# Norms of q and k from Gram matrices, and one folded projection in place of two projections and their maps

## The chip, the cores and the metric

The kernel runs on one core of one Trainium2 chip. The metric is the time of one execution on the device, in microseconds: the median of several runs. Profiles are of one execution, taken by the hardware profiler; their span runs from the first to the last instruction and is a little shorter than the time of the same execution.

## What is computed

A graph layer over 2500 nodes of 1024 features: normalise the rows of x, add to x a graph convolution (a sparse 2500 x 2500 matrix of 42500 weighted edges times xn @ W) and a mixing term, and then a feed-forward block with ternary weights. The change is in the mixing term:

```python
def _L0_mix_ref(x, Wq, bq, Wk, bk, Wv, bv, weights):      # x: normalised rows
    q = (x @ Wq.T + bq).reshape(Bx, Sx, H, D)              # 16 heads of 64
    k = (x @ Wk.T + bk).reshape(Bx, Sx, H, D)
    v = (x @ Wv.T + bv).reshape(Bx, Sx, H, D)
    q = q / jnp.linalg.norm(q)                             # one norm over the whole tensor
    k = k / jnp.linalg.norm(k)
    def phi(t):
        sq_norm = jnp.sum(t * t)
        scale = jnp.exp(-sq_norm / 2) / jnp.sqrt(jnp.float32(M))
        return jnp.exp(jnp.einsum('hmd,bshd->bshm', weights, t)) * scale
    phi_q = phi(q)
    phi_k = phi(k)
    s = jnp.einsum('bshm,bshm->bsh', phi_q, phi_k)[..., None]
    out = s * v / s
```

The norms are single numbers, so |q|^2 is a sum over all entries of (xn' xn) times (Wq' Wq), with the bias as one more column. And phi_q times phi_k is one exponential of the sum of both maps, so once the norms are known, map, projection and norm of q and of k can be folded into one 1024 x 1024 matrix.

## The kernel before

A tile is 125 rows of x (TILES = 20); KT = 8 blocks of 128 features. Matrix products in fp32 accuracy are made of three fp32r products, of a high and a low part of each operand (product3: lines 333, 334, 335). The high part is a copy on ACT, the low part a subtraction on DVE, 1 to 1.2 us for a tile each. PE takes its work strictly in the written order, as do ACT, DVE, POOL and SP (which issues most DMAs); semaphores tie them.

Stage 1 (0 to 107 us): SP loads x, DVE takes the row statistics (L952) and scales the rows (L963), PE transposes them (L1277), ACT copies the transposed tile into one of four slots of XT (L724), SP writes it out as xnT (L428). A slot is free when its store has landed. Stage 2 (to 627 us): groups of four tiles (500 rows) come back as xg. For q, then for k, for each of 5 groups and 8 blocks of heads: 24 products of 500 columns give a block of q (PS banks 4 and 5), ACT adds the bias, makes its high part and the sum of its squares (L761, L762), DVE the low part (L1000), three products with the block-diagonal maps bdH, bdL follow one block later (maps), and ACT and SP write the result u to DRAM (uT). The weights Wq and Wk are transposed by PE in the same stretch. Then the norms, a few tiny operations in a chain. Stage 3 (to 894 us): per tile 48 products of 512 columns give xn @ W (tile_products), kept in S; beside it u of q and k come back (uu), ACT takes exponentials, DVE multiplies, and PE sums over the 64 maps with eight products of 2 columns (map_sums, L1382) into s_all. Stage 4 (to 1146 us): Wv is loaded and transposed, v for each tile, times s, over s. Stage 5 (to 1707 us): the graph convolution as a dense product with A, which is read back from DRAM. Stage 6: the feed-forward block.

Beside stages 1 to 4, the dense A is built: POOL fills two matrices with zeros (40 strips of 1280 KB, L682), DVE compares the keys of each pair of 128-edge chunks (edge_pair, L345 to L350: four operations, 168 pairs) to sum edges that fall on one cell, and POOL scatters the sums with 336 indirect DMAs (L698), alternating between the two matrices; a matrix takes its next pair once its last has landed. Before stage 5 all of it must be done.

Of the kernel before, what the change touches and what calls it, by code (L numbers as in the profile page):

```python
# [32 lines left out]
P = 128  # L33
# [21 lines left out]
AHEAD = 2  # L55
PER_IT = 4
ITERS = 2 * GROUPS
BLOCKS = AHEAD + PER_IT * ITERS
CHUNKS = BLOCKS * CH_BLOCK
ROWS_C = CHUNKS  # L60
assert CHUNKS * P >= EDGES
CT = ROWS_C // 4

# [4 lines left out]
S_AT = W_AT + 2 * 4 * KT * D  # L68
# [11 lines left out]
def layer_kernel(nc, x, src, dst, edge_weight, W, Wq, bq, Wk, bk, Wv, bv, mix_w, w_gate, w_up, w_down, out):  # L80
# [5 lines left out]
    uT_d = nc.dram_tensor("uT", (2, P, KT, NODES), F32).ap()  # L86
# [22 lines left out]
    sel = small("sel", [P, 2])  # L109
    eps = small("eps", [P, 1])  # L110
    neg_round = small("neg_round", [P, 1])
    bqk = small("bqk", [P, 2, KT])
# [5 lines left out]
    ssq = small("ssq", [P, 2 * GROUPS * KT])  # L118
# [27 lines left out]
    w1 = zone("W1", W_AT, S_AT)  # L146
    XT = w1("XT", [P, GT, KT, ROWS])
    iedge = w1("iedge", [P, 2, ROWS_C], I32)
    kT_sb = w1("kT_sb", [P, 8, P])


    X = zone("S1", S_AT, E_AT)("X", [P, TILES, D])
    s2 = zone("S2", S_AT, E_AT)
    xg = s2("xg", [P, GT, KT, ROWS])
    xgH = s2("xgH", [P, 2, KT, GN], F32R)
    xgL = s2("xgL", [P, 2, KT, GN], F32R)
    S = zone("S3", S_AT, E_AT)("S", [P, TILES, D])


    e1 = zone("E1", E_AT, END_AT)  # L160
    wst = e1("wst", [P, 2, D])
# [3 lines left out]
    bdH = e1("bdH", [P, KT, P], F32R)  # L165
    bdL = e1("bdL", [P, KT, P], F32R)
    at = cursor["E1"]
    XN = zone("E1a", at, END_AT)("XN", [P, 2, D])
    e1b = zone("E1b", at, END_AT)
    qH = e1b("qH", [P, 2, GN], F32R)  # L170
    qL = e1b("qL", [P, 2, GN], F32R)
    usb = e1b("usb", [P, 2, GN])
    zeros = e1b("zeros", [P, A_PITCH // 4])
    squares = e1b("squares", [P, 2, GN], BF16)


    zx = zone("E2x", E_AT, END_AT)("zx", [P, 2, D])
# [4 lines left out]
    bvb = e2("bvb", [P, D])  # L182
    rows2 = zone("E2r", cursor["E2"] - 4 * D, END_AT)("rows2", [P, D])
    at = cursor["E2"]
    e2a = zone("E2a", at, END_AT)
    uu = e2a("uu", [P, 2, 2, 2, GN])
    rows3 = zone("E2s", cursor["E2a"] - 4 * 4 * GN, END_AT)("rows3", [P, 2, D])
    e2b = zone("E2b", at, END_AT)
    rs_all = e2b("rs_all", [P, TILES, HEADS])
# [3 lines left out]

# [8 lines left out]
    rq16 = e3("rq16", [P, TILES, D], BF16)  # L202
    Araw = e3("Araw", [P, 2, GN])
    AH = [e3(f"AH{i}", [P, GN], F32R) for i in range(2)]
    AL = [e3(f"AL{i}", [P, GN], F32R) for i in range(2)]

# [28 lines left out]
    Q_BLOCKS = ITERS * KT // 2  # L235
# [13 lines left out]
    s_exp = sems("s_exp", 2)  # L249
# [1310 lines left out]
```

## Time and profile before

| | us |
|---|---|
| median of 3 runs | 1879.35 |
| lowest, highest | 1879.14, 1879.56 |
| the profiled execution | 1875.68 |
| its span | 1873.9 |
| TensorE busy in the span | 1739.3 |
| VectorE (DVE) busy | 1101.7 |
| ScalarE (ACT) busy | 652.7 |
| GpSimd (POOL) busy | 578.4 |

PE is the matmul row, PEld the loads of its stationary operand, which overlap it. "Granted clock" is TensorE's clock as a share of 2.4 GHz; the other of its two levels is 1.2 GHz. Matmuls are pipelined, so the distance between two starts is what one costs, not its duration. A time in square brackets behind a row is how long the engine was idle before it, and what released it. A DMA share of 1 means that all 16 DMA engines were occupied.

### The profile page before, as it was taken

Reading aid. Unit: us, or ns where it says so; the run is one execution under the profiler, and the core shown is the slowest. Engines: PE = TensorE matmul, PEld = TensorE weight load, DVE = VectorE, ACT = ScalarE, POOL = GpSimd, SP = SyncE. Lnnn points to the kernel's source line nnn. Section 1 sums busy time; section 2 is a strip of 40 time slices with the busy share of each in tenths; the row PEclk is TensorE's granted clock in tenths of the full one; section 3 lists DMA queues with packets and bytes.
Section 4 is the critical chain, followed back from the end, with each engine's and each line's share of the span. In section 5 each row is a group of like instructions: output and inputs, shape, how many; then the busy total and the mean of one; then the engine's idle time right before and its main releaser. Section 6 shows DMA issues by size and latency. Waiting matters only on the chain.

```text
span 1873.9 us, 25902 instructions
## 1 busy us (share of the span) xinstructions
PE 1739.3 (93%) x8020; PEld 1390.9 (74%) x8020; DVE 1101.7 (59%) x2583; ACT 652.7 (35%) x937; POOL 578.4 (31%) x392
## 2 busy tenths in 40 slices
PE   2379999999999899999799999899999999999797
PEld 2368788888888688888677777677777777777465
DVE  5476777877777622222456664448566584755765
ACT  1243333443333533333322221223333343333443
POOL 1011111277787787877766700000000000000000
PEclk9689999999999899999999999899999999999899
DMA  8989999976666745545787756524545344453355
GB/s 204 324 353 379 384 382 380 380 189 164 160 161 165 233 99 131 124 107 132 182 247 212 201 176 178 163 90 140 131 131 139 91 142 131 131 142 99 113 165 160
DMA packets 176137, 356.75 MB, mean 190 GB/s; under 512 B 63979, under 2 KB 112139, under 8 KB 176091
## 3 DMA queue, kind: packets, MB, share of 16 engines
q1 hardware_dynamic: 109591, 278.48, 46.1%
q0 software_dynamic: 59264, 52.62, 13.0%
q10 hardware_dynamic: 7236, 25.12, 4.6%
q8 instruction: 19, 0.31, 0.1%
q14 instruction: 27, 0.22, 0.0%
HBM read 238.62 MB, written 117.53 MB: 190 GB/s over the span
## 4 chain that ended last, share of the span: by engine, by line
PE 82%; DMA 6%; DVE 5%; SPq 3%; ACT 2%; issue 1%; POOL 0%; ACTq 0%; DVEq 0%; POOLq 0%
PE PS L333 25%; PE PS L335 25%; PE PS L334 24%; PE PS L1493 4%; PE PS L1518 2%; DMA uT<-usb 2%; PE PS L1382 2%; DMA xnT<-XT 1%; PE PS L1277 1%; SPq L77 1%; SPq L417 1%; DMA ewrow<-weight_rows 1%; DMA Aside<-A_dense 1%; DVE junk L345 1%; ACT hqT L904 1%
## 5 line engine op out<-in xcount | busy, mean ns | idle before, releaser
L698 POOL DMA_INDIRECT A_dense<-wtot,cell x336 | 541.9, 1613 | 183.2 <-issue 100.7
L333 PE MATMUL PS<-SL,AH 125*125 125x512 f32 x800 | 317.6, 397 | 12.0 <-DVE AL L1133 11.9
L335 PE MATMUL PS<-SH,AH 125*125 125x512 f32 x800 | 318.0, 397 | 0.0
L334 PE MATMUL PS<-SH,AL 125*125 125x512 f32 x800 | 316.2, 395 | 0.0
L333 PE MATMUL PS<-WL,xtH 128*125 128x512 f32 x640 | 257.0, 402 | 4.8 <-DVE WL L1068 2.7
L333 PE MATMUL PS<-xgL,WH 128*128 (+1 forms) x640 | 250.7, 392 | 4.7 <-issue 4.7
L335 PE MATMUL PS<-WH,xtH 128*125 128x512 f32 x640 | 253.6, 396 | 0.0
L334 PE MATMUL PS<-WH,xtL 128*125 128x512 f32 x640 | 252.8, 395 | 0.0
L334 PE MATMUL PS<-xgH,WL 128*128 (+1 forms) x640 | 250.0, 391 | 0.0
L335 PE MATMUL PS<-xgH,WH 128*128 (+1 forms) x640 | 249.6, 390 | 0.0
L1130 DVE TENSOR_TENSOR SL<-S,SH 125x1024 fp32r<-125x1024 f32 x100 | 122.3, 1223 | 169.9 <-ACT SH L843 169.9
L843 ACT ACTIVATE SH<-S 125x1024 fp32r (+1 forms) x100 | 106.0, 1060 | 315.7 <-PE PS L335 315.7
L333 PEld LDWEIGHTS PS<-SL,AH 125*125 125x125 f32 x800 | 149.1, 186 | 50.7 <-DVE AL L1133 14.1
L334 PEld LDWEIGHTS PS<-SH,AL 125*125 125x125 f32 x800 | 149.3, 187 | 38.9
L335 PEld LDWEIGHTS PS<-SH,AH 125*125 125x125 f32 x800 | 149.3, 187 | 38.1
L345 DVE SCALAR_TENSOR_TENSOR junk<-keyrow,key,ewrow 128x256 bf16<-128x256 f32 x336 | 148.7, 479 | 4.1 <-DMA ewrow<-weight_rows 4.1
L761 ACT ACTIVATE qH<-PS,bqk 128x500 fp32r<-128x500 f32 x80 | 54.2, 678 | 267.2 <-PE PS L335 267.2
L333 PEld LDWEIGHTS PS<-WL,xtH 128*125 128x125 f32 x640 | 119.6, 187 | 33.7 <-issue 4.9
L333 PEld LDWEIGHTS PS<-xgL,WH 128*128 128x128 f32 x640 | 121.4, 190 | 30.1 <-issue 4.9
L335 PEld LDWEIGHTS PS<-WH,xtH 128*125 128x125 f32 x640 | 119.3, 186 | 30.1
L334 PEld LDWEIGHTS PS<-WH,xtL 128*125 128x125 f32 x640 | 119.8, 187 | 28.3
L335 PEld LDWEIGHTS PS<-xgH,WH 128*128 128x128 f32 x640 | 121.1, 189 | 25.2
(149 smaller groups left out, 2224.8 us busy)
## 6 DMA issues: line engine op xcount, KB each, us to landing
A_dense<-zeros POOLq DMA_DIRECT2D x40, 1280.0 KB, 11.0
Araw<-A_dense SPq DMA_DIRECT2D x100, 250.0 KB, 2.7
Aside<-A_dense SPq DMA_DIRECT2D x100, 250.0 KB, 2.9
xg<-xnT SPq DMA_DIRECT2D x11, 2000.0 KB, 14.1
uu<-uT SPq DMA_DIRECT2D x44, 500.0 KB, 4.5
keyrow<-key_rows SPq DMA_DIRECT2D x42, 512.0 KB, 4.9
ewrow<-weight_rows SPq DMA_DIRECT2D x42, 512.0 KB, 6.9
xt<-xnT SPq DMA_DIRECT2D x42, 500.0 KB, 5.1
```

The source lines that it names most:

```text
L77: eng.dma_start(dst[cut:ROWS], src[cut:ROWS]).then_inc(sem, 16)
L333: nc.tensor.matmul(o, lh, rl, start=start, stop=False)
L334: nc.tensor.matmul(o, ll, rh, start=False, stop=False)
L335: return nc.tensor.matmul(o, lh, rh, start=False, stop=stop)
L345: nc.vector.scalar_tensor_tensor(junk[:, slot, 2 * c:2 * c + 2, :].rearrange("p a n -> p (a n)"), row, key[:, col], wrow, ALU.is_equal, AL ...
L698: pool.indirect_dma_start(cells[m], bass.IndirectOffsetOnAxis(cell[:, col:col + 1], 0), wtot[:, col:col + 1], None, compute_op=ALU.add).th ...
L761: nc.scalar.activation(qH[:, j % 2, :], PS[:, 4 + j % 2, 0:GN], ACT.Identity, bias=bias)
L843: nc.scalar.activation(SH[0:ROWS, i, :], S[0:ROWS, bass.ds(s, 1), :].rearrange("p o n -> p (o n)"), ACT.Copy).then_inc(s_s[i], 1)
L1130: nc.vector.tensor_tensor(SL[0:ROWS, i, :], S[0:ROWS, bass.ds(s, 1), :].rearrange("p o n -> p (o n)"), SH[0:ROWS, i, :].bitcast(F32), ALU. ...
L1382: last = nc.tensor.matmul(PS[0:ROWS, 4 + jj, 2 * d:2 * d + 2], uu[:, i, jj, 0, d * ROWS:(d + 1) * ROWS], sel[:, :], start=True, stop=True)
L1493: last = nc.tensor.matmul(PS[0:ROWS, 2 * i + c, :], rqT[:, i, k, 0:ROWS], wT[:, c, :, k * P:(k + 1) * P], start=k == 0, stop=k == KT - 1)
L1518: last = nc.tensor.matmul(PS[0:ROWS, 4 + c, :], hqT[:, i, k, 0:ROWS], down_blocks(c, k), start=k == 0, stop=k == INNER // P - 1)
```

## The change

1. Stage 1 keeps the scaled rows in X and makes, right behind each tile's transposes, the left half of the Gram matrix xn' xn (gram with G_LEFT, banks 0 to 3; only blocks on and above the diagonal, with two more columns for the sums of the columns). High and low parts of a tile lie in ring, three slots. A second pass over the 20 tiles makes the right half (G_RIGHT). ACT copies the banks to Gs.
2. The same for the rows of Wq and Wk (raw, split in high and low parts into split), untransposed; DVE multiplies those banks with Gs and sums (weigh), which gives both norms.
3. The maps, scaled by the norms (bdqk), times the rows of Wq and Wk give one matrix: 128 + 16 fp32 products (fold), into TH and TL.
4. One more pass of tile_products with TH and TL, in front of W's, gives the exponents of both maps together; DVE adds the bias, ACT takes the exponential, DVE sums over each head. u, uT, uu, xg, the maps' products and map_sums are gone.
5. The order around it: SP loads x first and the biases as rows of 512 bytes; POOL starts its strips of zeros at once (four free, then one per Gram item), twenty pairs of edges go to A[0] alone while A[1] is zeroed; the edge pairs on DVE follow a table of pairs per step; the rows of Wv come in parts, the most of them during the last tiles of W's pass.

The core of the diff:

```diff
+G_LEFT = [(0, 0, 512, 0, 0), (0, 512, 1024, 1, 0), (1, 128, 640, 2, 0), (1, 640, EXT, 3, 0), (0, D, EXT, 3, 386)]
+G_RIGHT = [(2, 256, 768, 0, 0), (2, 768, EXT, 1, 0), (7, 896, EXT, 1, 258), (4, D, EXT, 1, 388), (3, 384, 896, 2, 0),
+           (3, 896, EXT, 3, 0), (6, 768, EXT, 3, 130), (4, 512, 1024, 4, 0), (5, 640, EXT, 5, 0)]
+EDGE_PLAN = [1] * TILES + [0, 0, 0, 0, 1, 1, 1, 1] + [0, 1, 1, 0, 1, 1, 0, 1] + [1, 0, 1, 0, 1, 0, 1, 1] \
+    + [1, 1, 1, 1, 1, 1, 0, 0] + [4] + [2] * KT + [3] * (TILES - KT) + [4] * 18 + [0] * 2
...
     @block.sync
+        sp.wait_ge(s_st, 6)
+        for n in range(6):
+            load_raw(n, s_raw[0])
         for t in range(TILES):
             sp.wait_ge(s_xev[t % 2], t // 2 + 1)
             sp.dma_start(xnT_d[t].rearrange("p k r -> p (k r)"), XT[:, t % GT].rearrange("p k r -> p (k r)")).then_inc(s_xTout[t % GT], 16)
...
     @block.gpsimd
+        for r in range(STRIPS):
+            if r >= 4:
+                pool.wait_ge(s_gm, r - 3)
+            zero_strip(0, r)
+        for i in range(2):
+            pool.wait_ge(s_Azero[i], 16 * (STRIPS // 2))
+        for r in range(STRIPS):
+            zero_strip(1, r)
+            scatter_pair(r, 0)
...
     @block.scalar
+        for n in range(TILES):
+            if n % 2 == 0 and n + 2 < TILES:
+                deviations(n // 2 + 1)
+            high_of_rows(n + 1)
+            transposed_rows(n)
...
     @block.vector
+        dve.wait_ge(s_gm, ITEMS)
+        weigh(1, K_RIGHT, RIGHT_WIDTHS, 4)
...
+        for t in range(TILES):
+            i = t % 2
+            low_of_tile(1 - i, t // 2 + i)
+            if t < KT:
+                dve.wait_ge(s_w2h, t + 1)
+                nc.vector.tensor_tensor(WL[:, t, :], stage[:, t % 2, :], WH[:, t, :].bitcast(F32), ALU.subtract).then_inc(s_w2l, 1)
+            dve.wait_ge(s_mm[i], t // 2 + 1)
+            if t >= 2:
+                dve.wait_ge(s_red[i], t // 2)
+            nc.vector.tensor_tensor(ex[0:ROWS, i, :], two_banks(i)[0:ROWS], bb[0:ROWS, :], ALU.add).then_inc(s_ta[i], 1)
+            edges(STEP_T + t)
+            dve.wait_ge(s_ex[i], t // 2 + 1)
+            nc.vector.tensor_reduce(s_all[0:ROWS, t, :], ex[0:ROWS, i, :].rearrange("p (h n) -> p h n", h=HEADS), AX.X,
+                                    ALU.add).then_inc(s_red[i], 1)
...
     @block.tensor
+        def gram(segments, banks, hi, lo, first, last_one):
+            opened = set()
+            for i, a, b, bank, at in segments:
+                o = PS[:, banks[bank], at:at + b - a]
+                cols = slice(i * P, (i + 1) * P)
+                nc.tensor.matmul(o, hi[:, cols], lo[:, a:b], start=first and bank not in opened, stop=False, skip_group_check=True)
+                opened.add(bank)
+                nc.tensor.matmul(o, lo[:, cols], hi[:, a:b], start=False, stop=False, skip_group_check=True)
+                last = nc.tensor.matmul(o, hi[:, cols], hi[:, a:b], start=False, stop=last_one, skip_group_check=True)
+            last.then_inc(s_gm, 1)
...
+        def fold(lhs_of, rows, slot):
+            for j in range(KT):
+                for m in range(2):
+                    last = nc.tensor.matmul(by_block(two_banks(2 + slot))[0:rows, j, :], lhs_of(m * KT + j), bdqk[:, m, j, :],
+                                            start=m == 0, stop=m == 1)
+            last.then_inc(s_fold, 1)
...
+        with pe.Fori(0, HALF) as h:
+            for i in range(2):
+                pe.wait_ge(s_xtl[i], h + 1)
+                pe.wait_ge(s_ta[i], h)
+                tile_products(i, TH, TL)
```

On PE, the transposes of stage 1 stand before in a loop over pairs of tiles, and the transposes of two weight blocks and the products of stage 2 follow once it is done (XN is the scaled tile, wst two slots for rows of a weight matrix, xgH, xgL and WH, WL the parts of four tiles and of the weights):

```order
L1277 MATMUL PS<-ident_49,XN_95 128x128 x16
L1291 REGISTER_ALU
L1291 COMPARE_AND_BRANCH
L1277 MATMUL PS<-ident_49,wst_89 128x128 x16
L333 MATMUL PS<-xgL_87,WH_79 128x500
L334 MATMUL PS<-xgH_86,WL_80 128x500
L335 MATMUL PS<-xgH_86,WH_79 128x500
```

In the changed kernel, PE's first tile reads so, and the next follows at once:

```order
L1294 MATMUL PS<-ident_49,X_85 128x125 x8
...
L1281 MATMUL PS<-ring_83 128x512
L1278 MATMUL PS<-ring_83 128x386
L1280 MATMUL PS<-ring_83 128x386
L1281 MATMUL PS<-ring_83 128x386
L1278 MATMUL PS<-ring_83 128x2
L1280 MATMUL PS<-ring_83 128x2
L1281 MATMUL PS<-ring_83 128x2
L1294 MATMUL PS<-ident_49,X_85 128x125 x8
```

Fifteen Gram products stand now between the transposes of two tiles, and three of them have 2 columns.

On SP before, between the last loads of x and the first keys' rows:

```order
L76 DMA X<-in_x 112x4x1024
L77 DMA X<-in_x 13x4x1024
L417 DMA bqk<-in_L_mix_bq 128x8x1
L417 DMA bqk<-in_L_mix_bk 128x8x1
L391 DMA wst<-in_L_mix_Wq 128x1024 [waits s_tr0]
L391 DMA wst<-in_L_mix_Wq 128x1024
L428 DMA xnT<-XT 128x1000 [waits s_xev0]
```

And in the changed kernel:

```order
L97 DMA X<-in_x 112x2x1024
L98 DMA X<-in_x 13x2x1024
L437 DMA raw<-in_L_mix_Wq 128x1024 [waits s_st]
L437 DMA raw<-in_L_mix_Wq 128x1024 x5
L445 DMA xnT<-XT 128x1000 [waits s_xev0]
```

The first store of xnT still stands behind all of x; in between stand six weight blocks where two were, and the biases have moved up in front of the fourth pair of tiles.

On PE again, what stands between the last Gram product and the first tile of the added pass (norms are the two sums, earlier a block of ones, brow the folded bias):

```order
L1281 MATMUL PS<-split 128x386
L1344 MATMUL PS<-norms,earlier 128x2
L1349 MATMUL PS<-bdqk,raw 128x128 x128
L1349 MATMUL PS<-bdqk,raw 2x128 x16
L1365 MATMUL PS<-brow,earlier 128x512 x2
```

Nothing of PE's other work is left to stand beside the norms: the fold reads the scaled maps, and the pass behind it the folded matrix.

## Rows read from the trace of the kernel before

**Rows 1.** The page: the span, and shares of the chain that ended last.

```profile
span 1873.9 us, 25902 instructions
...
PE 82%; DMA 6%; DVE 5%; SPq 3%; ACT 2%; issue 1%; POOL 0%; ACTq 0%; DVEq 0%; POOLq 0%
```

**Rows 2.** By stretch: length; busy PE, PEld, DVE, ACT, POOL; clock; DMA share; GB/s.

```profile
30.00:60.00 30.00, 8.52 (x45) 7.85 (x43) 15.32 (x31) 4.21 (x5) 0.00 (x0) 0.67 0.93 207
60.00:107.00 47.00, 23.79 (x128) 21.22 (x129) 26.14 (x45) 22.11 (x25) 2.38 (x3) 0.68 0.87 331
...
200.00:320.00 120.00, 119.91 (x530) 99.33 (x529) 88.48 (x377) 43.32 (x85) 14.24 (x20) 1.00 0.99 379
```

**Rows 3.** The same view in stretches of 10 us.

```profile
20.00:30.00 10.00, 1.08 (x5) 1.08 (x6) 6.98 (x15) 1.58 (x2) 0.00 (x0) 1.00 1.05 250
...
110.00:120.00 10.00, 10.00 (x46) 8.33 (x45) 9.86 (x55) 2.26 (x4) 0.71 (x1) 0.90 1.02 417
```

**Rows 4.** Timeline of stage 1: start, length, engine, operation, idle before and releaser.

```profile
20.83 4.84 DVE L952 BATCH_NORM_STATS2 stats<-X 125x6 f32<-125x512 f32 x8 [5.67 <-DMA X<-in_x]
...
33.05 18.03 SPq L417 DMA_DIRECT2D bqk<-in_L_mix_bk  x1
...
57.77 2.37 SPq L428 DMA_DIRECT2D xnT<-XT  x4
...
64.34 1.00 ACT L724 ACTIVATE XT<-PS 128x1000 f32<-128x1000 f32 x1 [25.34 <-DMA xnT<-XT]
```

**Rows 5.** Timeline of PE in stage 2, five products apart.

```profile
616.71 0.39 PE L333 MATMUL PS<-xgL,WH 128*128 x1
...
617.84 0.38 PE L335 MATMUL PS<-xgH,WH 128*128 x1
```

**Rows 6.** Timeline of PE in stage 3, around the map sums of a tile.

```profile
653.79 0.39 PE L333 MATMUL PS<-WL,xtH 128*125 128x512 f32 x1
...
660.72 1.80 PE L1382 MATMUL PS<-sel,uu 128*125 128x2 f32 x16
...
662.38 0.48 PE L333 MATMUL PS<-WL,xtH 128*125 128x512 f32 x1
```

**Rows 7.** The chain in order of time: start, length, work.

```profile
137.08 0.81 DVE junk L345 x4
138.56 0.81 DVE junk L345 x4
...
326.75 0.88 PE PS L1277 x8
...
660.88 1.64 PE PS L1382 x16
673.76 1.64 PE PS L1382 x16
```

**Rows 8.** Groups by line: operands, count, busy us, mean ns, idle before.

```profile
L1130 DVE TENSOR_TENSOR SL<-S,SH 125x1024 fp32r<-125x1024 f32 x100 | 122.3, 1223 | 169.9 <-ACT SH L843 169.9
...
L1000 DVE SCALAR_TENSOR_TENSOR qL<-PS,bqk,qH 128x500 fp32r<-128x500 f32 x80 | 58.9, 736 | 82.2 <-ACT squares L762 82.1
...
L963 DVE TENSOR_SCALAR XN<-X,mv,rstd 125x1024 f32<-125x1024 f32 x20 | 15.8, 811 | 9.3 <-PE PS L1277 9.1
...
L1356 PE MATMUL PS<-norms,earlier 128*128 128x2 f32 x2 | 0.5, 330 | 3.2 <-DVE norms L1030 3.2
```

**Rows 9.** Timeline of PE from the last map sums to the first product of v.

```profile
894.46 1.94 PE L1277 MATMUL PS<-ident,wst 128*128 128x128 f32 x16 [0.52 <-issue]
...
903.82 3.63 PE L1277 MATMUL PS<-ident,rows 128*128 128x128 f32 x16 [4.76 <-DMA rows<-in_L_mix_Wv]
...
909.07 0.47 PE L333 MATMUL PS<-WL,xtH 128*125 128x512 f32 x1
```

**Rows 10.** All scatters of POOL: count, ns min/median/max, first and last start.

```profile
L698 POOL DMA_INDIRECT A_dense<-wtot,cell x336: 1538/1541/2557, 362.1 to 1073.9; - x168
```

**Rows 11.** DMA issues, the strips of zeros: count, KB each, us to landing.

```profile
A_dense<-zeros POOLq DMA_DIRECT2D x40, 1280.0 KB, 11.0
```

More of the change, by code:

```diff
@@ L477, in load_tile, with load_w_rows @@
+        next_key_rows(0, STEP_Q)
+        sp.wait_ge(s_gm, G_ITEMS)
+        for n in range(10, 2 * KT):
+            load_raw(n, s_raw[2])
+        def load_w_rows(k):
+            sp.dma_start(stage[:, k % 2, :], W[k * P:(k + 1) * P, :]).then_inc(s_stage[k % 2], 16)
+        sp.wait_ge(s_lo, G_ITEMS)
+        for k in range(2):
+            load_w_rows(k)
+        next_key_rows(STEP_Q, STEP_FOLD)
         def load_tile(t, i):
@@ L702, in _ @@
+        for pair in range(ALONE, BLOCKS * PAIRS):
+            scatter_pair(pair, (pair + 1) % 2)
     @block.scalar
     def _(act):
[L704 to L709 removed]
@@ L777, in _ @@
-        stage2_group(0, 0, own=True)
-        with act.Fori(1, GROUPS - 1) as g:
-            stage2_group(0, g)
-        stage2_group(0, GROUPS - 1, ahead=True)
-        stage2_group(1, 0)
-        with act.Fori(1, GROUPS) as g:
-            stage2_group(1, g)
-        evacuate_u(ITERS - 1, KT - 1)
+        act.wait_ge(s_ev0, 4)
+        nc.scalar.activation(raw[:, 0:KT, D:EXT], bias[:, 0], ACT.Copy).then_inc(s_ev0, 1)
+        act.wait_ge(s_ev0, 5)
+        act.wait_ge(s_lo, G_ITEMS)
+        for j in range(2):
+            high_of_weights(0, j)
@@ new lines, in _ @@
+        act.wait_ge(s_gm, G_ITEMS)
+        evacuate_gram(RIGHT_BANKS, RIGHT_SCALES, 4, (0, 1))
+        high_of_weights(0, 2)
+        evacuate_gram(RIGHT_BANKS, RIGHT_SCALES, 4, (2, 3))
+        high_of_weights(0, 3)
+        evacuate_gram(RIGHT_BANKS, RIGHT_SCALES, 4, (4, 5))
+        nc.scalar.activation(raw[:, KT:2 * KT, D:EXT], bias[:, 1], ACT.Copy).then_inc(s_ev0, 1)
+        for j in range(4, KT):
+            high_of_weights(0, j)
+        act.wait_ge(s_ev0, 6)
+        for j in range(KT):
+            high_of_weights(1, j)
@@ new lines, in _ @@
+        for j in range(KT):
+            edges(STEP_K + j)
+        dve.wait_ge(s_gm, G_ITEMS + 3 * KT)
+        weigh(1, K_LEFT, LEFT_WIDTHS, 0)
+        for j in range(KT):
+            edges(STEP_K + KT + j)
+        dve.wait_ge(s_gm, ITEMS)
+        weigh(1, K_RIGHT, RIGHT_WIDTHS, 4)
+        dve.wait_ge(s_bs, 20)
+        dve.wait_ge(s_rs, 2)
+        nc.vector.tensor_reduce(norms[:, 0, :], parts[:, :, :], AX.X, ALU.add).then_inc(s_norm, 1)
+        dve.wait_ge(s_norm, 3)
+        nc.vector.reciprocal(norms[:, 2, :], norms[:, 1, :]).then_inc(s_norm, 1)
@@ new lines, in _ @@
+        pe.wait_ge(s_bdq, 2)
+        for k in range(KT):
+            if k == 1:
+                pe.wait_ge(s_norm, 5)
+            if k >= 2:
+                pe.wait_ge(s_fl, k - 1)
+            fold(lambda n: raw[:, n, k * P:(k + 1) * P], P, k % 2)
+        pe.wait_ge(s_fl, KT - 1)
+        fold(lambda n: raw[:, n, D:EXT], 2, 0)
+        pe.wait_ge(s_fl, KT)
+        pe.wait_ge(s_bb, 1)
+        for c in range(2):
+            last = nc.tensor.matmul(PS[:, 6 + c, :], earlier[0:1, 0, :], brow[0:1, c * 512:(c + 1) * 512], start=True, stop=True)
```

928 lines of the change are left out of this document (416 added, 512 removed).

## The prediction

> **What bounds the kernel now.** I read the page first: the chain that ended last is PE for 82% of the span of 1873.9 us [rows 1]. So time is gained only where PE does less or waits less. The table by stretch then says where it waits: busy for 8.5 of the 30 us from 30 to 60 and 23.8 of the 47 us from 60 to 107, at a granted clock of 0.67 and 0.68, against 119.9 of 120 us at 1.00 (the 2.4 GHz level) from 200 to 320 [rows 2]. So there are two prices: PE time after 107 us counts in full, PE time before it is mostly free. Why the first 107 us are idle shows in the timeline: the first xnT store goes out at 57.77, behind all of x and two bias loads that hold SP's queue for 18 us, and ACT copies tile 4 only at 64.34 [rows 4].
>
> **Unit prices.** Products of 500 columns start 0.226 us apart (616.71 to 617.84, five steps) [rows 5], of 512 columns 0.231 (653.79 to 660.72, 30 products) [rows 6]. Between them the width alone acts, so I price 386 columns at 0.178 and 258 at 0.125 (500 less the columns at 2.4 GHz). The trace shows no fp32r product under 500 columns. Below, its bound is a weight load alone: 16 records of 2 columns take 1.66 us, 0.104 each [rows 6]; above, the price of a 512-column one, 0.231. For 2 columns I take 0.104, for 130 columns 0.11, the price of a transpose of 128 columns (8 in 0.88 us) [rows 7]. The page "TensorE: Matmul & The Clock Gate" of the Trainium skill (section "Back-to-back issue gap") gives 81 ns for a streamed product of 128 columns; by it the 216 products of 130 columns would cost 6 us less in all; the transposes here show 110 ns, and the sum goes by them.
>
> **The change, part by part.** I compare one milestone: the start of the first transpose of Wv, now at 894.46 [rows 9]. Behind it the program is the same but for one wait.
>
> *Left Gram pass over x, in stage 1.* Per tile 15 products: 3 x (3 x 0.231 + 0.178 + 0.104) = 2.93 us, with 8 transposes 3.81. DVE needs per tile 1.21 (statistics, 8 in 4.84 [rows 4]) + 0.81 (scaling) + 1.22 (low part) [rows 8] = 3.3, ACT two copies of 1.0 [rows 4]: both under PE. But the first xnT store again stands last in SP's queue: x (10.24 MB at 235 to 250 GB/s [rows 3], 43 us) and six weight blocks (3.1 MB, 8 to 12 us), so it lands no sooner than 55 to 58. Beside it POOL now zeroes A from the start: ten strips may go before tile 6, 1.31 MB each [rows 11], 3.1 us at 417 GB/s [rows 3], up to 31 us of the same engines. ACT waits for that landing at tile 4, and PE at tile 6 waits for ACT. The stall ends between 57 and 88; I take 72, about the middle. From there 14 tiles x 3.81 = 53, and 7 for a cold start and the chain through ACT: the pass ends at **132** (117 to 148). The section "Queues, rings and completion order" of "DMA: Bandwidth & Descriptors" in the Trainium skill says that a DMA engine takes turns between queues, packet by packet; by it the strips get their full share and the pass ends near 148. No row of before has x and strips together.
>
> *Right pass.* Per tile 27 products: 3 x (3 x 0.231 + 2 x 0.125 + 2 x 0.11 + 0.104 + 0.178) = 4.34; 20 tiles are **86.8**, after 1.8 us in which ACT empties two banks. DVE's share per tile, 1.22 [rows 8] and an edge pair of 1.5 us (137.08 to 138.56 [rows 7]), hides.
>
> *Gram of the weights.* Twice 8 x (2.93 + 4.34): **116.3**. In front of each of the four parts PE waits for banks: 2.0 (ACT), 1.8 (two weighings at 0.74 [rows 8]), 5.3 (last high part on ACT 1.0 [rows 4], low 1.22, an edge pair 1.5, two weighings), 2.2: **11.3**.
>
> *Norms.* Six weighings of about 0.69, reduction, ones product, root, reciprocal and two scalings of the maps at 0.8 (as the scaling of a tile [rows 8]): **8.0**, all with PE idle.
>
> *Folding.* 144 fp32 products of 128 columns, each two records as in L1356 (x2) [rows 8]: from 2 x 0.104 to 2 x 0.231. I take 0.225, two transposes: 32.4, and 4 for the cold clock, 3 for the bias row: **39.3** (to 73 at the upper bound).
>
> *Projection.* 20 x 48 = 960 products more, at 0.232: **222.5**, and W's own pass **222.5** now that the map sums are gone from it (a tile took 12.88 us, 660.88 to 673.76 [rows 7]). DVE has about 8.5 us of work per tile beside 11.1 (three edge pairs, 4.5, and three whole-tile operations and flags, 4.0): it hides, but with two more edge pairs it would set the pace.
>
> Sum: 132 + 1.8 + 86.8 + 116.3 + 11.3 + 8.0 + 39.3 + 445 + 0.5 = **841**, against 894.5: 53.5 us. What this replaces is not listed apart; it is all that stands between 107 and 894.46, above all 2160 products of 500 columns (488 us) and 33 us of map sums.
>
> *Boundary to Wv.* PE waits 4.76 us for rows [rows 9]; now rows 2 to 6 come during the last two tiles of W, since uu no longer takes the room. That wait and a little of the rhythm behind it go: 5.5. What is late next is DVE's 1.22 per block, already in the rhythm.
>
> *Scatter.* 336 scatters took from 362.1 to 1073.9 [rows 10], 2.12 us each. Now the first pairs follow at about 150, but twenty of them go to one matrix and alternate with strips; while W's pass runs, DVE offers 72 pairs faster (four per tile of 11.1) than POOL takes them (4.24 each), so POOL ends about 305 us behind the start of that pass at 616, near 920. The loads of A stand in front of the last two tiles of v, near 1065: it hides, with 140 us to spare.
>
> The whole: 53.5 + 5.5 = 59 us. The profiled execution took 1875.68 (span 1873.9), so 1816.7; the median of before, 1879.35, lies 3.7 above that execution: **1820**.
>
> **Rivals.** (a) *Products of 130 columns cost four passes*, as fp32 takes more than one record for its product: 0.234 in place of 0.11, 216 times: 27 us, **1847**. For it: nothing narrow in fp32r is in the trace. Against it: the transposes. (b) *Four passes up to 258 columns too*: 216 x (0.124 + 0.323) = 96.5 us, **1916**. This is the way to end slower. The price is PE's alone, in right passes over x and weights; it decides as soon as the narrow products together cost 59 us more than I charge, which 130 columns alone can't reach and 258 do. Against it: from 512 to 500 columns the price falls with the width. (c) *The DMA stall in stage 1 is not there*: x and strips overlap, xnT lands before PE needs tile 6, the pass ends at 99: **1787**. For it: 417 GB/s are moved from 110 to 120 us, x alone moves 250, so engines that look full have room. Against: x alone showed a share of 1.05.
>
> **How the numbers follow.** Forecast 0.56, (a) 0.25, (b) 0.05, (c) 0.12, the fold at its upper bound or a wait that I overlook by itself 0.02 beyond the range. The range, 1794 to 1860, takes in pass ends from 117 to 148 and rival (a) with some of the fold's upper bound; most of (c) and all of (b) are left out. A difference of about 0.2% (4 us) is what a measurement can tell from none. Faster 0.93: all but (b) and a little. Same 0.01, slower 0.06.
>
> **What would show it.** Spacing of the products by width: 512 at 0.231, 258 at 0.125, 130 at 0.11 (a right item at 4.34, a left one at 2.93). ACT's wait for xnT at its fifth copy, ending near 72, and PE idle from about 45 to 75. The first product of W's pass near 616, the first transpose of Wv near 841. The fold's 128 products in 29 us. POOL's last scatter before the loads of A. I am wrong where a right item takes over 5 us, where the stall goes or lasts beyond 88, or where tiles of the projection take over 11.3 us because DVE or the loads of xt come late.

## The result, and the profile after

| | before | after |
|---|---|---|
| median of 4 executions, us | 1879.24 (1879.09 to 1879.56) | 1820.91 (1818.56 to 1824.12) |
| profiled execution, its time / its span, us | 1875.68 / 1873.9 | 1823.07 / 1821.3 |
| PE busy in it | 1739.3 us (93%) | 1705.3 us (94%) |
| instructions | 25902 | 23768 |

The ratio is 0.969 (95% interval 0.967 to 0.971): 58.3 us less by the medians. By the profiled executions it is 52.6 us of span, since that of before lay 3.6 us under its median and that of after 2.2 us above its own. The steps below are compared within the profiled executions.

The page of after: the span, PE in 40 slices of 45.5 us with the granted clock, and the engines of the chain that ended last; it answers [rows 1].

```profile
span 1821.3 us, 23768 instructions
...
PE   5199998899999999999999997999999999999797
...
PEclk9599999999999999999999998999999999999899
...
PE 88%; DMA 3%; DVE 3%; SPq 3%; issue 1%; ACT 1%; DVEq 0%; ACTq 0%
```

PE's share of the chain rose from 82% to 88%. Apart from the first slice, in which the first rows arrive, the one hole is in the second: "1" for PE, "5" (the 1.2 GHz level) for its clock. By stretch (length; busy PE, PEld, DVE, ACT, POOL; clock; DMA share; GB/s), to be held against [rows 2]:

```profile
30.00:46.00 16.00, 14.70 (x93) 13.01 (x92) 9.03 (x16) 5.57 (x8) 1.67 (x2) 1.00 1.02 414
46.00:83.00 37.00, 0.82 (x7) 0.74 (x5) 1.34 (x4) 2.46 (x3) 3.35 (x4) 0.54 0.99 393
83.00:140.00 57.00, 56.23 (x324) 50.07 (x324) 43.13 (x73) 30.46 (x39) 7.54 (x9) 0.94 0.91 348
141.00:228.00 87.00, 87.00 (x540) 78.90 (x540) 53.47 (x178) 21.86 (x24) 43.12 (x30) 1.00 0.82 270
403.00:850.00 447.00, 447.00 (x1924) 357.25 (x1925) 300.70 (x1157) 86.58 (x89) 310.38 (x196) 1.00 0.55 132
```

From 46 to 83 us no engine is busy for more than a tenth of the time (PE for 0.82 of 37 us), while the DMA engines are full. In the right pass (141 to 228) and in the two passes over 20 tiles (403 to 850) PE is busy all the time. The hole in the timeline of stage 1 (start, length, engine, line, operation, idle before and what ended it), as [rows 4] showed it for before:

```profile
37.26 14.96 SPq L437 DMA_DIRECT2D raw<-in_L_mix_Wq  x6
...
52.26 34.80 SPq L445 DMA_DIRECT2D xnT<-XT  x7
80.54 1.00 ACT L698 ACTIVATE XT<-PS 128x1000 f32<-128x1000 f32 x1 [39.25 <-DMA xnT<-XT]
...
83.74 1.93 PE L1294 MATMUL PS<-ident,X 125*128 125x125 f32 x8
```

The first xnT store leaves SP's queue at 52.26, behind x and the six raw weight blocks, and lands 28 us later. ACT's fifth copy waits for it, PE for that copy. What shared the DMA engines, by queue from 46 to 81 us (packets, MB, share of the 16 engines; q1 is SP's queue, q0 the queue of POOL, which zeroes A):

```profile
q1 hardware_dynamic: 2058, 7.44, 53.3%
q0 software_dynamic: 1638, 6.38, 45.3%
```

The price of a product by its width, from an item of the right pass: three products each of 512, 258, 130 and 2 columns.

```profile
180.63 0.40 PE L1281 MATMUL PS<-ring 125*128 125x512 f32 x1
180.87 0.28 PE L1278 MATMUL PS<-ring 125*128 125x258 f32 x1
...
181.22 0.23 PE L1278 MATMUL PS<-ring 125*128 125x130 f32 x1
181.28 0.28 PE L1280 MATMUL PS<-ring 125*128 125x130 f32 x1
181.40 0.28 PE L1281 MATMUL PS<-ring 125*128 125x130 f32 x1
181.51 0.22 PE L1278 MATMUL PS<-ring 125*128 125x2 f32 x1
...
181.81 0.48 PE L1278 MATMUL PS<-ring 125*128 125x512 f32 x1
182.13 0.39 PE L1280 MATMUL PS<-ring 125*128 125x512 f32 x1
182.36 0.40 PE L1281 MATMUL PS<-ring 125*128 125x512 f32 x1
...
184.50 0.39 PE L1278 MATMUL PS<-ring 125*128 125x512 f32 x1
```

Three of 258 columns take 0.35 us from start to start (0.118 each), three of 130 columns 0.29 (0.097), three of 2 columns 0.30 (0.10). The average of three hides how they lie: over the 35 triples of 130 columns in this pass the second product starts 0.06 us behind the first, and the next two starts follow at 0.110 and 0.112 to 0.113 (0.28 us in all); behind the first of three products of 2 columns the distances are 0.079, 0.112 and 0.112. So from 130 down to 2 columns the distance no longer falls. Where the 258 columns follow 130, their three take 0.41 us instead of 0.35. The item ends at 184.50, 4.33 us after its first product at 180.17. The first 512-column product behind the narrow ones holds the next one back to 0.32 us.

Last, the boundary to Wv, against [rows 9], and the scatters, against [rows 10]:

```profile
849.65 1.91 PE L1269 MATMUL PS<-ident,zx 128*128 128x128 f32 x16
853.29 2.19 PE L1269 MATMUL PS<-ident,keyrow 128*128 128x128 f32 x16 [1.73 <-DVE WL L1062]
...
858.77 0.47 PE L354 MATMUL PS<-WL,xtH 128*125 128x512 f32 x1
```

```profile
L662 POOL DMA_INDIRECT A_dense<-wtot,cell x336: 1533/1542/2517, 157.3 to 988.9; - x168
```

The 4.76 us wait for rows is gone; two waits for DVE (1.73 and 1.34 us) stand in this stretch. The last scatter starts at 989 instead of 1074.

### The profile page after: what moved, and what is told of

It reads as the page before. It is cut to its first block, busy times and chain, and to the rows that moved or that the text cites. A ratio compares the mean times of both kernels' runs of the same rounds, so it can differ in the third digit from the quotient of the medians.

```text
span 1821.3 us, 23768 instructions
## 1 busy us (share of the span) xinstructions
PE 1705.3 (94%) x8178; PEld 1372.3 (75%) x8178; DVE 1097.2 (60%) x2537; ACT 513.7 (28%) x610; POOL 580.5 (32%) x392
## 4 chain that ended last, share of the span: by engine, by line
PE 88%; DMA 3%; DVE 3%; SPq 3%; issue 1%; ACT 1%; DVEq 0%; ACTq 0%
PE PS L356 22%; PE PS L355 22%; PE PS L354 22%; PE PS L1280 5%; PE PS L1278 5%; PE PS L1281 5%; PE PS L1491 4%; PE PS L1516 2%; PE PS L1349 2%; DMA xnT<-XT 2%; DMA Aside<-A_dense 1%; SPq L98 1%; SPq L437 1%; PE PS L1294 1%; ACT hqT L884 1%
## 5 line engine op out<-in xcount | busy, mean ns | idle before, releaser
L354 PE MATMUL PS<-WL,xtH 128*125 128x512 f32 x640 | 252.6, 395 | 2.7 <-DVE WL L1062 2.7
L355 PEld LDWEIGHTS PS<-SH,AL 125*125 125x125 f32 x800 | 149.6, 187 | 37.4
L354 PE MATMUL PS<-TL,xtH 128*125 128x512 f32 x320 | 127.1, 397 | 0.0
L356 PE MATMUL PS<-TH,xtH 128*125 128x512 f32 x320 | 126.9, 397 | 0.0
L355 PE MATMUL PS<-TH,xtL 128*125 128x512 f32 x320 | 126.3, 395 | 0.0
L1022 DVE TENSOR_TENSOR xtL<-xt,xtH 128x1000 fp32r<-128x1000 f32 x61 | 73.1, 1198 | 75.1 <-ACT xtH L767 74.6
L1278 PE MATMUL PS<-ring 125*128 125x512 f32 (+4 forms) x280 | 95.4, 341 | 4.8 <-DVE ring L934 3.4
L934 DVE TENSOR_TENSOR ring<-X,ring 125x1024 fp32r<-125x1024 f32 x40 | 48.7, 1217 | 84.7 <-ACT ring L692 84.7
```

The source lines that it names most:

```text
L354: nc.tensor.matmul(o, lh, rl, start=start, stop=False)
L355: nc.tensor.matmul(o, ll, rh, start=False, stop=False)
L356: return nc.tensor.matmul(o, lh, rh, start=False, stop=stop)
L1022: nc.vector.tensor_tensor(xtL[i][:, :, :], xt[:, i], xtH[i][:, :, :].bitcast(F32), ALU.subtract).then_inc(s_xtl[i], 1)
L1278: nc.tensor.matmul(o, hi[:, cols], lo[:, a:b], start=first and bank not in opened, stop=False, skip_group_check=True)
```

## The experiments

All times are medians. The kernel before stood beside every group at 1879 to 1880 us.

**The base, once more.** No edit.

> The changed kernel as it is, as the base of this group. Both theories: 1818 to 1824 us, PE idle from about 47 to about 83 us in stage 1, the store of tile 0 landing near 80 us. A question beside it: its runs so far lie near 1818.6 or near 1823.5 us; if the difference sits in one stage, a second profile should show that stage 4 to 5 us shorter or longer than the first.

Measured: 1824.0 us (1820.4 to 1824.6), 3.1 above the median of the first group. The hole lies at the same place, but ACT waits until 82.8 instead of 80.5, and the left pass ends 1.9 us later. This profile again fell among the longer executions, so what shortens the others by 4 to 5 us isn't seen in one. Their mean granted clock is 0.977 to 0.978 against 0.974 to 0.975; the clock experiment below comes back to it.

**Who delays the store: three edits.** First, the strips of zeros wait for the left pass:

```diff
-            if r >= 4:
-                pool.wait_ge(s_gm, r - 3)
+            pool.wait_ge(s_gm, max(7, r - 3))
```

> The zero strips of the first half of A from number 4 on wait until left tile 7 is through PE (before: strip r waits for left tile r-4), so that GpSimd's queue moves nothing in 52 to 81 us. The queue of the strips moved 6.38 of 14.10 MB in 46 to 81 us. Theory (the store waits behind what shares the DMA engines with it): q1 alone moves what stands ahead of the store, some 6 MB, at up to 400 GB/s, so the store of tile 0 lands near 65 to 70 us instead of 80, and the time falls by 10 to 15 us, to about 1808. Rival (q1 by itself is no faster than with the strips beside it: in 10 to 30 us, before the strips, it moved 324 to 344 GB/s or less): it lands at 72 or later and the gain is under 8 us.

Measured: 1806.3 us, 17.7 less than the base. Timeline of ACT, then 50 to 60 us by stretch:

```profile
62.86 1.00 ACT L697 ACTIVATE XT<-PS 128x1000 f32<-128x1000 f32 x1 [22.41 <-DMA xnT<-XT]
```

```profile
50.00:60.00 10.00, 0.00 (x0) 0.00 (x0) 0.00 (x0) 0.00 (x0) 0.00 (x0) 0.50 1.01 360
```

The store lands 18 to 20 us sooner, for two reasons: it is issued at 40.6 instead of 52 to 54 us (SP's own issues get through faster), and then needs 22 instead of 28 us. The rival falls: SP's queue alone moved 3.44 of the 3.60 MB of this stretch, 344 GB/s, 1.6 times the 213 GB/s (7.44 MB in 35 us) that it had beside the strips. So the strips cost the changed kernel some 18 us; I had expected 10 to 15. One number of the expectation was misread: the 324 to 344 GB/s in 10 to 30 us of the changed kernel were not SP's queue before the strips, since the strips moved 3.40 of the 6.68 MB there.

Second, the six raw weight blocks go behind the loop of the stores:

```diff
-        for n in range(6):
-            load_raw(n, s_raw[0])
         for t in range(TILES):
...
             sp.wait_ge(s_xTout[i], 16 * GROUPS)
+        for n in range(6):
+            load_raw(n, s_raw[0])
         for n in range(6, 10):
```

> The six raw weight loads (3.1 MB) are issued behind all stores of x tiles instead of ahead of them. Theory (bytes ahead in SP's queue set the landing): at 210 GB/s for q1 beside the strips, 3.1 MB are 15 us, so the store of tile 0 lands near 65 us, and the time falls by 12 to 15 us, to about 1807. Rival (SP's issue of the raw loads, 37 to 52 us, is what delayed the store, not their bytes): the store is issued at about 42 instead of 52 us and still takes 28 us: it lands near 70, a gain of about 10 us. Second rival (the rest of stage 1 then runs into the late weights): the gain is lost again before the Q projection's Gram pass, total within 3 us of the base.

Measured: 1812.4 us (1804.9 to 1817.2), 11.6 less. The store is issued at 37.5 and lands at 66.2, as long under way (29 us) as before. It lands where the theory put it, its flight is that of the first rival: the two are not told apart. The second rival falls: PE waited for no load in the Gram pass of the weights. That pass did take 134.2 us from the start of its first product to that of its last, against 129.0 in the base, at a mean clock of 0.92 against 0.96, a matter taken up below.

Third, the stores leave SP's queue:

```diff
@@ sync
-            sp.wait_ge(s_xev[t % 2], t // 2 + 1)
-            sp.dma_start(xnT_d[t]..., XT[:, t % GT]...).then_inc(s_xTout[t % GT], 16)
@@ scalar, behind the copy of tile n
+            act.wait_ge(s_xev[n % 2], n // 2 + 1)
+            act.dma_start(xnT_d[n]..., XT[:, n % GT]...).then_inc(s_xTout[n % GT], 16)
```

> The stores of the x tiles are issued on ScalarE's DMA queue, each right behind the evacuation that it stores, instead of on SP's; nothing else moves. Theory (the stall of 36.6 us is a queue that the store stands in, nothing that PE or ScalarE needs): the store of tile 0 lands within 5 to 12 us of its issue at about 34 us, PE is never idle over 5 us in a row, the left pass ends near 105 us instead of 139, and the time falls by 25 to 36 us, to 1785 to 1796. Rival (in this stretch all 16 DMA engines are full, so whatever is taken out of one wait comes back in the next, the loads of x and of the raw weights): the left pass ends at 120 or later and the gain is under 18 us. On ScalarE the issues cost 20 x about 0.1 to 0.5 us, at 36% load: nothing on the path.

The keys' first rows were loaded from inside the loop that goes away on SP; they are now issued right behind the raw weights, so a little more moves than the expectation says.

Measured: 1790.9 us (1789.6 to 1795.0), 33.2 less than the base. The store of tile 0 is issued at 19.5 us and has landed 8.2 us later, where it took 28 us in SP's queue. By stretch:

```profile
40.00:50.00 10.00, 10.00 (x63) 8.87 (x62) 9.41 (x16) 5.70 (x8) 0.84 (x1) 1.00 1.03 407
50.00:60.00 10.00, 10.00 (x60) 8.84 (x59) 9.04 (x17) 2.42 (x4) 1.25 (x2) 1.00 1.03 409
60.00:70.00 10.00, 6.31 (x24) 5.14 (x24) 2.14 (x2) 4.31 (x5) 1.27 (x2) 0.66 1.03 421
```

PE is busy where it stood idle for 37 us; the DMA engines are as full as before. So the stall was the store's place in a queue, and the rival falls: most of the bytes on the engines were not what PE needed. The left pass ends at 105.3, as expected; one hiccup of 4 us remains at 60 to 66 us, where ACT waits 9.0 us for a store. That is the fifth store, issued at 40.7 us, which took 22 us on this queue too.

**All three together.**

> The three edits of the first group together: the stores of the x tiles on ScalarE's queue, the zero strips of the first half of A from number 4 on behind left tile 7, the raw weights behind SP's other work of stage 1. The store version alone ran at 1790.9 us, with stores still landing 8 to 22 us after their issue, and ScalarE waiting 21.9 us in all for them. Theory (the waits of ScalarE for the stores that remain are shared DMA engines, and PE follows them): they fall to under 8 us, the left pass ends about 8 us sooner, 1780 to 1786 us. Rival (what is left of stage 1 is bound by VectorE, 3.5 to 3.8 us for each tile, and the waits are slack): within 3 us of 1790.9. Third case: strips and weights that start later meet the loads of the right pass, and it is slower than 1794.

Measured: 1789.6 us (1784.3 to 1793.3). No copy of ACT waits for a store any more, and the last transposes of x start at 96.1 instead of 102.4. But the gain is eaten twice, as the third case had it in part. In the right pass an edge pair waits for its rows, which now travel with strips and raw weights:

```profile
DVE junk L366 <- DMA ewrow<-weight_rows: 12.1, 1, 12.1
```

PE loses 4.3 us behind it, and its clock is at 0.57 in the ten microseconds that follow (144 to 154 us). And the Gram pass of the weights takes 132.9 us from first to last product instead of 126.8, though it does the same work: the clock was at its lower level for 17 us of it, against 3.4 us in the version with the stores alone.

**Narrow products twice.** Two segments of 130 columns stand twice in the list:

```diff
-            (7, 896, EXT, 1, 258), ... (3, 896, EXT, 3, 0), ...
+            (7, 896, EXT, 1, 258), (7, 896, EXT, 1, 258), ... (3, 896, EXT, 3, 0), (3, 896, EXT, 3, 0), ...
```

> Two of the narrow segments of every right item, 130 columns each, are issued twice, which adds 6 products to each of 36 items, 216 in all (the sums of these two blocks count double, so the output changes). Theory (a narrow product costs its weight load, 0.097 us from start to start in the profile): +21 us, 1842 to 1848 against 1821 to 1824, all of it on PE. Rival (a product under 256 columns costs four passes in fp32r, 4 x 130 columns, about 0.23 us): +50 us, 1871 or more. Second rival (the right pass waits for VectorE or ScalarE, so that PE time in it is partly free): under +12 us.

Measured: 1850.1 us (1844.8 to 1853.1), 26 more than the base. Of two neighbouring triples of 130 columns in its trace:

```profile
140.63 0.27 PE L1278 MATMUL PS<-ring 125*128 125x130 f32 x1
140.74 0.27 PE L1280 MATMUL PS<-ring 125*128 125x130 f32 x1
140.85 0.27 PE L1281 MATMUL PS<-ring 125*128 125x130 f32 x1
140.96 0.22 PE L1278 MATMUL PS<-ring 125*128 125x2 f32 x1
```

0.11 us apart. The right pass over x grew from 87.0 to 100.2 us: 13.2 for 120 products, 0.110 each, 24 us for the 216. The rival with four passes (+50) falls, and the one with free PE time (+12) too. Its profiled execution is 21 us above the base's, the other three are 26 to 29 above; these 5 us aren't explained by the product's price; the mean granted clock of those three is 0.971 to 0.974 against its 0.978.

**A light left pass.**

```diff
-            gram(G_LEFT, LEFT_BANKS, ...)
+            gram(G_LEFT if n in (0, TILES - 1) else G_LEFT[4:], LEFT_BANKS, ...)
```

> In left tiles 1 to 18 only the last segment of 2 columns is multiplied (3 of 15 products); tiles 0 and 19 stay whole. The Gram matrices' left halves are then wrong, the output changes; 216 products, 18 x about 3.1 us of PE time from start to start are gone, no load, store or evacuation changes. Theory (the left pass is set by the stall up to 83 us, and behind it by PE at 3.79 us a tile against VectorE at about 3.5): the 5 tiles before the stall give nothing, the 13 behind it 0.2 to 0.4 us each, a gain of 3 to 6 us, at most 10. Rival (PE sets the left pass throughout): 50 us. Between: if VectorE can run ahead as far as the ring lets it, 10 to 25 us.

Measured: 1815.1 us, 9.0 less than the base, where PE lost 47 us of work (18 tiles of 9 x 0.232 + 3 x 0.178 us; the 3.1 us a tile in my expectation was too much). By stretch, behind the stall:

```profile
90.00:100.00 10.00, 5.82 (x27) 5.43 (x28) 9.46 (x16) 6.19 (x8) 1.68 (x2) 0.50 1.01 378
100.00:110.00 10.00, 7.93 (x39) 7.55 (x38) 9.67 (x17) 5.88 (x8) 0.84 (x1) 0.50 1.01 354
```

DVE is busy for 95% and 97% and sets the pace; PE idles a third of the time at 1.2 GHz. So of these 47 us some 38 are hidden, in the stall or beside DVE. The measured gain is at the upper end of what I expected. The granted clock was at its lower level from 31 to 133 us here, so part of what looks hidden may have gone into slower products; this version doesn't separate the two.

**Is it the old kernel's stall too?** Two versions of the kernel before: first, the two scattered bias loads stand behind the first group's stores (four of them; my text of expectation said ten, wrongly); second, also the stores are issued on ACT's queue, by the two lines shown above.

```diff
-            for i, v in enumerate((bq, bk)):
-                sp.dma_start(bqk[:, i, :], ...).then_inc(s_bias, 16)
...
             if t == GT - 1:
+                for i, v in enumerate((bq, bk)):
+                    sp.dma_start(bqk[:, i, :], ...).then_inc(s_bias, 16)
```

> The kernel before with one edit: the two scattered loads of biases (4-byte pieces), whose issue held SP's queue for 18.03 us at 33 us, are issued behind the first ten stores of x tiles. It shows what of the change's gain the new form of the biases' load gave. Theory (the stall of 25.3 us in the kernel before started with this issue): the load pairs behind it and the store of tile 0 come up to 18 us sooner, bounded by the bytes ahead of them: the time falls by 6 to 12 us, 1867 to 1873. Rival (the same bytes still stand ahead of the store and the DMA engines are full from 30 us on): under 3 us.

Measured: 1877.4 us (10 executions), ratio to before 0.9993 (0.9983 to 1.0004): nothing. The rival holds. The first store is now issued at 33.8 instead of 57.8 us, and ACT waits to almost the same moment as in [rows 4]:

```profile
62.40 1.00 ACT L724 ACTIVATE XT<-PS 128x1000 f32<-128x1000 f32 x1 [24.12 <-DMA xnT<-XT]
```

> The kernel before with the stores of the x tiles on ScalarE's DMA queue, and the scattered loads of biases at the end of SP's list for stage 1 instead of ahead of it. It asks how much of what stage 1 holds belongs to the old kernel too. Theory (stage 1 of both kernels stands behind the store of tile 0; the old one lost 25.3 us in one wait, of 36.4 in all): the first product of stage 2 starts at 80 to 92 us instead of 107.6 and the time falls by 15 to 27 us, to 1852 to 1864. Rival (the loads of x, 224 to 254 GB/s in this stretch with all DMA engines full, set stage 1 of the old kernel; late biases alone gave 1.7 us): under 8 us.

Measured: 1867.0 us, ratio 0.993 (0.991 to 0.996), 12.9 less than the 1880.0 beside it; stage 2 starts at 94.8 instead of 107.0. Between the theory and the rival. The same edit is worth 33 us in the changed kernel and 13 in the old one.

Why less there? Not by the loads of x, as the rival had it. Waits of ACT and of DVE from 20 to 96 us (for what; us in total, times, longest):

```profile
ACT XT L722 <- DMA xnT<-XT: 8.9, 6, 2.1
...
DVE stats L952 <- DMA X<-in_x: 5.2, 1, 5.2
```

DVE waits for x once here, before its first group of tiles (until 20.3 us), and not again in stage 1. ACT's waits for stores fell from 36.4 to 8.9 us. What is left of stage 1 is engines waiting for each other: ACT 20.5 us for PE, DVE 10.8 us for PE and 5.6 us for ACT. The last tile's transposes start 18 us sooner (81.0 instead of 99.0), but the first product of stage 2, which needs the stored tiles back, comes 13.8 us behind them instead of 8.0.

**Stores on ACT, strips late.** The first and the third edit of the group above, without the second.

> The changed kernel with the stores on ScalarE's queue and the zero strips behind left tile 7, the raw weights where they were. The version that also had the raw weights late had one 12 us wait of VectorE for rows of edge weights (DMA) in the right pass, 4.3 us of it on PE. Theory: this wait goes, the left pass ends near 98 us as there, and the whole is 4 to 8 us under the 1790.9 us of the store version: 1783 to 1787. Rival (its left pass ends at 105 us, as with the stores alone): within 2 us of 1790.9.

Measured: 1790.1 us (1785.4 to 1794.5): nothing gained over the stores alone. The last product of the right pass did start at 192.4 instead of 197.4, and the Gram pass of the weights then took 132.9 instead of 126.8 us. Where it loses, by stretch:

```profile
220.00:225.00 5.00, 5.00 (x22) 4.53 (x22) 0.55 (x3) 0.00 (x0) 3.68 (x3) 0.59 0.65 172
225.00:230.00 5.00, 5.00 (x25) 4.40 (x24) 1.23 (x1) 1.06 (x1) 3.35 (x4) 0.72 0.74 208
```

PE waited 1.6 us at the boundary from Q left to Q right, and behind that the clock is 0.59 and 0.72 for ten microseconds: 22 and 25 products in 5 us, where 33 or 34 are normal. In the version with the stores alone, the same wait left the clock at 1.00. Of the nine traces of changed kernels in which this wait of 1.6 us stands unfilled, the clock falls within 2 us behind it in six and stays up in three.

**Filling the waits.**

```diff
+        def junk(count, bank):
+            for i in range(count):
+                nc.tensor.matmul(PS[:, bank, 0:P], ident[:, :], ident[:, :], start=True, stop=True)
...
+                        pe.wait_ge(s_gev, 13)
+                        junk(5, 6)
                         pe.wait_ge(s_gev, 20)
...
+                        pe.wait_ge(s_bs, 4)
+                        junk(19, 4)
                         pe.wait_ge(s_bs, 6)
...
+        pe.wait_ge(s_bs, 14)
+        junk(14, 6)
         pe.wait_ge(s_norm, 1)
```

> The same, with products of the identity by itself, written to banks that are free at that point, in three places where PE waits: 5 (about 1.2 us) at the wait between Q left and Q right, 19 (4.5 us) at the 5.2 us wait ahead of K left, 14 (3.3 us) at the 3.9 us wait ahead of the norms. Behind these waits the granted clock was at the lower level for some us: 0.68 to 0.83 in 255 to 265 us, 0.50 in 295 to 300 us, 0.55 in 365 to 370 us in the changed kernel; products there started 0.4 us apart instead of 0.23. Theory (the clock falls because PE stands idle): it stays at 1.00 from the left pass to the projection, and 6 to 9 us go. Rival (the clock falls for another reason, or the added products push the work behind them): within 2 us of the version without them, or slower by up to 3 us.

Measured: 1783.3 us (1782.2 to 1787.3), 6.8 less than without; the slowest here and the fastest there (1785.4) overlap. The same place as above in its trace:

```profile
224.00:229.00 5.00, 4.97 (x30) 4.52 (x31) 1.05 (x4) 0.28 (x1) 3.52 (x3) 1.00 0.72 199
229.00:234.00 5.00, 5.00 (x34) 4.56 (x33) 1.23 (x1) 1.75 (x2) 4.11 (x3) 1.00 0.55 135
```

The Gram pass of the weights takes 125.4 instead of 132.9 us. Not all of this is owed to the filling in every execution: with the stores alone, where the clock mostly stayed up by itself, the pass took 126.8 us. Three drops remain up to the projection: 0.50 in 109 to 114 us, behind a 1.33 us wait between left and right pass, 0.66 in 330 to 335 us, behind the norms, and 0.80 in 365 to 370 us, behind the fold. Over the traces the length of this pass follows the time that the clock spent at its lower level in it: 125.4 us with none (this version), 126.8 with 3.4 us, 127.1 with 6.8, 129.1 with 10.2, 132.8 to 132.9 with 17.1, 134.2 with 20.5, always for the same 672 products.

The same in three more places, 5, 5 and 4 products:

```diff
+        junk(5, 4)
         for n in range(TILES, G_ITEMS):
...
+                        pe.wait_ge(s_gev, 6)
+                        junk(5, 2)
                         pe.wait_ge(s_gev, 11)
...
         pe.wait_ge(s_fl, KT)
+        junk(4, 6)
         pe.wait_ge(s_bb, 1)
```

> The version with added identity products, with three more places: 5 between the left and the right pass (a wait of 1.3 us), 5 between the right pass and Q left (1.35 us), 4 ahead of the biases' product behind the fold (1.2 us). Behind the first and the last the granted clock had been lower in the version before (0.50 in 109 to 114 us, 0.80 in 365 to 370 us), behind the middle one 1.00. Theory (short waits of PE, from about 1.2 us on, make the clock fall in part of the executions, and filling them prevents it): the clock is 1.00 in every 5 us from the left pass's end to the projection; 2 to 5 us under 1783.3: 1778 to 1781, and the executions lie closer together. Rival (only the waits of 4 and 5 us mattered, or the drop falls at a place that no wait explains): within 1.5 us of 1783.3.

Measured: 1784.6 us (1780.6 to 1787.5), no gain over the version before; the rival's number. The clock did what the theory said at the first place, and not at the last:

```profile
101.00:106.00 5.00, 4.89 (x36) 4.46 (x35) 4.31 (x13) 3.05 (x8) 0.84 (x1) 1.00 0.97 393
...
358.00:363.00 5.00, 4.99 (x13) 3.02 (x13) 4.78 (x27) 4.42 (x6) 4.39 (x3) 0.74 0.31 14
```

At 358 to 363 us PE was busy for 4.99 of 5.00 us and still had 0.74, and it was busy for 4.99 of the 5 us from 355 to 360 too, at 1.00: behind the fold a wait of PE isn't what lowers it. What does stays open. Behind the norms, where the wait is filled only in part, the clock fell as before (0.66 in 322 to 327 us). All five executions had the same mean clock, 0.990 to 0.991, and their spans still lie 6.9 us apart (1777.8 to 1784.7). So the clock isn't all of the spread between executions; the rest stays open.

The best kernel of the study is the one with the stores on ACT's queue, the strips late and three waits filled: 1783.3 us, ratio to before 0.948 (0.947 to 0.950), 2% under the changed kernel.

## Why the prediction was right, and where only its sum was

The forecast was 1820.0 us, the median is 1820.9. Its mechanism holds: PE does less work, the left Gram pass hides in part in the stall of stage 1, and the rest counts in full. That the forecast hits the median to 0.9 us is luck, since two errors cancel: the profiled span is 6.4 us longer than my sum's 1814.9 (1873.9 - 59), and the median of after lies 2.2 us below its profiled execution where that of before lay 3.6 above, which no step of the prediction foresaw. The milestones:

| step | forecast, us | measured, us |
|---|---|---|
| left pass ends | 132 (117 to 148) | 139.5 |
| right pass with its wait | 1.8 + 86.8 | 1.5 + 87.0 |
| Gram of the weights with its waits | 116.3 + 11.3 | 131.0 (228.0 to 359.0) |
| norms | 8.0 | 6.5 |
| fold and bias row | 39.3 | 37.4 |
| both passes over 20 tiles | 445.5 | 446.7 |
| first transpose of Wv | 841 | 849.65 |
| first transpose of Wv to the second block's first product, gained | 5.5 | 5.5 (24.9 to 19.4) |
| behind it, gained | 0 | 2.2 |

- *Left pass, the term that was mis-sized.* "I take 72, about the middle" for the landing of the first store. It was 80.5: the strips took 45% of the DMA engines' time and SP's queue 53%, and with the strips out of the way the store landed 18 to 20 us sooner. The section "Queues, rings and completion order" of "DMA: Bandwidth & Descriptors" in the Trainium skill says that an engine alternates between queues; these two shares agree. By it I had put the pass's end near 148, too late. A tile behind the stall took 3.79 us (forecast 3.81), and from the landing to the end of the pass it was 59 us (forecast 60). The 235 GB/s that I give as the lower rate of x stands in no row; over 20 to 50 us of the kernel before it was 216 to 250.
- *Product prices.* 0.232, 0.178, 0.118 and 0.10 for 512, 386, 258 and 2 columns against 0.231, 0.178, 0.125 and 0.104 (258 columns behind 130: 0.137). For 130 columns 0.094 to 0.097 as the mean of three, 0.110 to 0.112 once narrow ones follow each other (forecast 0.11). The item came out at 4.33 against 4.34: the 0.09 us lost by the product behind the narrow ones made up for the lower prices. Rivals (a) and (b), four passes, fall by the trace and by the doubled segments. The "Back-to-back issue gap" section of "TensorE: Matmul & The Clock Gate" in the Trainium skill has 81 ns for 128 columns; here three products of 130 columns took 94 to 97 ns each on average, and 110 to 112 ns from one to the next behind the first.
- *Gram of the weights.* 3.4 us over. The waits themselves were shorter than mine (1.35, 1.59, 5.24 and 1.50 us, 9.7 against 11.3). I had put down a cold clock only for the fold. In this execution it was at 0.68 in 255 to 260 us and at 0.50 in 295 to 300 us, each behind a wait that I had listed at its bare length. The pass took 129.1 us from first to last product here, and 125.4 in the version with its waits filled.
- *Norms and fold.* Both a little cheaper. The 144 products of the fold took 34.3 us against my 36.4. At the upper level of the clock one cost 0.223 (two records 0.112 apart; forecast 0.225); the first 18 records ran at the lower level, 0.222 apart, which cost 2 us where I had 4. The upper bound of 0.46 was far off.
- *Rival (c), no stall,* did not happen, but its price was nearly right: with the stores on another queue the kernel ran at 1790.9 us, against 1787.
- *The 2.2 us behind v* were not foreseen. 1.8 of them lie in the last stage (from the first to the last transpose of rq 145.7 us before, 143.9 after). The old kernel with late biases had 144.2 there, so this looks like spread between executions rather than the change.
- *Scatters* started at 157 us (forecast 150) and ended at 989 (920). When W's pass started, at 627 us (616), 162 of them were left instead of 144, and these took 2.23 us each instead of 2.12. The first load of A goes out at 1079 us (1065): hidden, with 90 us to spare instead of the 140 that I gave them.

## What to carry to other kernels

Where an early stage shows PE idle and the DMA engines full, ask what the awaited transfer stands behind: a store that frees a buffer belongs on a queue with nothing ahead of it, and that was worth more (33 us) than thinning the traffic around it. Moving work into such a hole is mostly free (38 of 47 us here), but traffic that is moved forward beside it, here strips of zeros, lengthens the hole (18 us). What such an edit is worth depends on what stands behind the wait: the same one gave 33 us in one kernel and 13 in the other. And a wait of PE costs more than its length when the clock falls behind it, so allow a few microseconds at the lower level behind waits of this kind.

## What the runs showed of the hardware

- A PE wait of 1.6 us between two full stretches was followed by a lower granted clock in six traces (in one of them 0.59 and 0.72 in the ten microseconds behind it) and not in three (1.00). Where it fell, 22 to 25 products started in 5 us instead of 33. An edit elsewhere can thus gain or lose some us with no change in the work: the Gram pass of the weights took 126.8 to 134.2 us for the same products, which blurred three of the experiments.
- With PE busy for 58% and 79% of two 10 us stretches, in the light left pass, the granted clock stayed at 0.50.
- x alone moved at 216 to 250 GB/s in 20 to 50 us of the kernel before with all engines at a share of 1.0 or above, and x, weights and strips together at 403 GB/s in the changed one. A share of 1.0 isn't the limit of what the engines move.
- The first 512-column product behind 2-column ones holds the next back to 0.31 to 0.32 us instead of 0.23.
- Between fp32r products that follow each other the distance falls with the width down to 258 columns (0.118 us) and then stays at 0.110 to 0.113 us, for 130 columns as for 2 (only the second product after a change of width comes sooner, 0.06 to 0.08 us behind the first). The two records of an fp32 product of 128 columns lie 0.112 us apart as well.
